# Index tiles for two halves by one transfer, and 25 rows of target scores in place of 22, in a graph attention kernel

## The reference, cut to what matters

```python
def gat_layer(feat, src, dst, W, a, gamma, beta):
    msg = feat @ W
    attn_src = msg @ a[:dh]
    attn_dst = msg @ a[dh:]
    scores = leaky_relu(attn_src[src] + attn_dst[dst], 0.2)
    e = exp(scores - scores.max())
    denom = segment_sum(e, dst, num_segments=n) + 1e-10
    out = segment_sum(msg[src] * (e / denom[dst])[:, None], dst, num_segments=n)
    ...
head_outs = [gat_layer(feat, src, dst, W_heads[h], ...) for h in range(8)]
x = gat_layer(concatenate(head_outs), src, dst, W_out, ...)
```

## Time and profile before

| | |
|---|---|
| median of 3 runs | 9308.34 us (9302.91 to 9314.57) |
| span of the profiled execution, first to last instruction | 7890.3 us |
| what the median has beyond this span | 1418.0 us |
| POOL busy, share of the span | 5124.5 us, 65% |
| DVE busy | 4825.2 us, 61% |
| PE busy | 5464.8 us, 69% |
| G0 (gathers start to next phase) | about 186 to 2296 us |
| G1 | about 2828 to 4990 us |

### The profile page before, as it was taken

One profiled execution on the slowest core, in us unless ns is written; L12 is line 12 of the kernel. 1 busy time (PEld: TensorE's weight loads), 2 busy tenths in 40 slices (PEclk: granted clock), 3 DMA queues, 4 the chain that ended last, 5 costly groups with the idle time before them and its releaser, 6 DMA issues.

```text
span 7890.3 us, 195306 instructions
## 1 busy us (share of the span) xinstructions
PE 5464.8 (69%) x50500; PEld 3952.8 (50%) x50501; DVE 4825.2 (61%) x14588; ACT 3085.2 (39%) x7615; POOL 5124.5 (65%) x4726
## 2 busy tenths in 40 slices
PE   3767677777773746777776777435878874888887
PEld 3655556565651336666666666323444442444444
DVE  7555555555556556666666666575666663555555
ACT  2111111111121135555555555413555552666665
POOL 1776767676740157777777777025887784777777
PEclk9977675656555855555555555567999996999999
DMA  3223232323233532222222222033555553544444
GB/s 122 57 56 77 56 77 56 77 56 77 56 76 125 148 47 52 52 51 51 51 51 51 51 51 51 12 91 95 124 124 125 124 125 92 120 116 118 118 118 107
DMA packets 600102, 647.29 MB, mean 82 GB/s; under 512 B 331121, under 2 KB 490355, under 8 KB 599665
## 3 DMA queue, kind: packets, MB, share of 16 engines
q0 software_dynamic: 190000, 384.58, 23.9%
q1 hardware_dynamic: 338379, 238.04, 10.4%
q10 hardware_dynamic: 71640, 23.81, 1.2%
HBM read 562.39 MB, written 83.23 MB: 82 GB/s over the span
## 4 chain that ended last, share of the span: by engine, by line
DVE 27%; issue 19%; POOL 15%; DMA 14%; PE 13%; DVEq 5%; ACT 3%; SPq 3%; ACTq 1%; POOLq 0%
POOL acc L659 8%; POOL rows L639 7%; DMA acc<-list_dst 7%; PE psa L1407 4%; PE psc L1366 3%; DMA rows<-t_gat,idx 2%; DVE acc L1729 2%; DVE acc L1781 1%; DMA acc<-in_x 1%; DVEq L619 1%; DMA acc<-y_d 1%; DVE acc L1728 1%; ACT ohb L1120 1%; PE psc L1498 1%; DVE s_m L1837 1%
## 5 line engine op out<-in xcount | busy, mean ns | idle before, releaser
L639 POOL DMA_INDIRECT rows<-t_gat,idx x3168 | 3142.8, 992 | 1189.8 <-issue 903.3
L659 POOL DMA_INDIRECT acc<-t_part,acc x1400 | 1826.6, 1305 | 546.6 <-issue 460.2
L1407 PE MATMUL psa<-rhs,rows 128*128 128x176 f32 (+1 forms) x6336 | 1713.1, 431 | 23.2 <-DVEq L1922 12.2
L1217 ACT ACTIVATE acc<-psa 128x384 bf16<-128x384 f32 x3200 | 1290.2, 506 | 884.7 <-PE psa L1481 765.8
L1407 PEld LDWEIGHTS psa<-rhs,rows 128*128 128x128 f32 x6336 | 1497.2, 311 | 132.0 <-DVEq L1922 83.2
L1481 PE MATMUL psa<-den,rhs 125*32 125x384 bf16 x12800 | 785.2, 343 | 191.4 <-ACT acc L1217 149.8
L1128 ACT ACTIVATE wgt<-s_d 128x64 f32<-128x64 f32 (+1 forms) x396 | 93.8, 237 | 1625.5 <-DVE s_d L1838 1610.8
L1122 ACT ACTIVATE oht<-psc 22x1024 bf16<-22x1024 bf16 x402 | 407.3, 1013 | 783.9 <-PE psc L1366 730.4
L1395 PE MATMUL psc<-oh,wgt 128*8 128x22 f32 (+1 forms) x6336 | 290.2, 205 | 552.1 <-ACT wgt L1128 543.8
L1071 ACT ACTIVATE acc<-stg,acc 128x128 bf16<-128x128 f32 x1818 | 552.9, 387 | 198.2 <-issue 116.0
L1481 PEld LDWEIGHTS psa<-den,rhs 125*32 125x32 bf16 x12800 | 285.6, 97 | 641.9 <-ACT acc L1217 412.7
(11 more groups left out here) (348 smaller groups left out, 7870.4 us busy)
## 6 DMA issues: line engine op xcount, KB each, us to landing
rows<-list_src SPq DMA_DIRECT2D x200, 500.0 KB
rows<-t_gat,idx POOLq DMA_INDIRECT x3168
acc<-y_d SPq DMA_DIRECT2D x50, 1000.0 KB, 5.0
y_d<-stg SPq DMA_DIRECT2D x100, 250.0 KB, 2.8
acc<-t_part,acc POOLq DMA_INDIRECT x1400
acc<-t_sage SPq DMA_DIRECT2D x300, 62.5 KB
adw<-win_d SPq DMA_DIRECT2D x820, 2.2 KB
adw<-win_d SPq DMA_DIRECT2D x788, 0.4 KB
```

The source lines that it names most:

```text
L639: eng.indirect_dma_start(rows[:, j, 0:spec["width"]], None, spec["table"], bass.IndirectOffsetOnAxis(ap=idx[:, j:j + 1], axis=0)).then_inc ...
L659: eng.indirect_dma_start(h_prow[u][:, t, :], None, t_parts[layer], bass.IndirectOffsetOnAxis(ap=h_idx[u][:, t:t + 1], axis=0)).then_inc(h_ ...
L1217: eng.activation(h_rows[:, g, :], psa[:, g % 4, 0:D3], ACT.Copy).then_inc(hyb["ev"], 1)
L1407: last = eng.matmul(sums(half, q, h), rows[:, slot * TH + j, 0:D], right, start=(j == 2 * q), stop=(j == 2 * q + 1))
```

## The change

One transfer now loads the indices of two slots (16 tiles, 64 bytes for each partition), issued in the odd slot after the rows of both have landed. Each semaphore `idx_in` stands for two slots, and POOL waits for it at the even slot only. The windows of `adw` are loaded with 25 rows (`WINL`); PE still uses the first 22. The tables in memory get three more rows at their end for it.

```diff
 WIN = 22
+WINL = 25
...
-        adw = sb("adw", [WIN, 2, PAIRS, 3 * K0], BF16)
+        adw = sb("adw", [WINL, 2, PAIRS, 3 * K0], BF16)
...
-                        eng.wait_ge(idx_in[slot], i * 16)
+                        if slot % 2 == 0:
+                            eng.wait_ge(idx_in[slot // 2], i * 16)
...
             def load_idx(slot, b):
-                eng.dma_start(idx[:, slot * TH:slot * TH + TH],
-                              src_t[:, ds(tile_at(spec, b, slot), TH)]).then_inc(idx_in[slot], 16)
+                eng.dma_start(idx[:, slot * TH:(slot + 2) * TH],
+                              src_t[:, ds(tile_at(spec, b, slot), 2 * TH)]).then_inc(idx_in[slot // 2], 16)
...
-                        eng.dma_start(adw[:, half, q, 0:3 * k], spec["window"][ds(at + s0, WIN), :]).then_inc(adw_in[half], 16)
+                        eng.dma_start(adw[:, half, q, 0:3 * k], spec["window"][ds(at + s0, WINL), :]).then_inc(adw_in[half], 16)
...
-                    eng.wait_ge(rows_in[spec["name"]][slot], value(eng, nb) * (16 * TH))
-                    load_idx(slot, eng.snap(nxt[1], min_val=0, max_val=(2 * SB - spec["slots"]) // spec["unit"]))
+                    if slot % 2:
+                        for read in (slot - 1, slot):
+                            eng.wait_ge(rows_in[spec["name"]][read], value(eng, nb) * (16 * TH))
+                        load_idx(slot - 1, eng.snap(nxt[1], min_val=0, max_val=(2 * SB - spec["slots"]) // spec["unit"]))
...
-            for slot in range(spec["slots"]):
+            for slot in range(0, spec["slots"], 2):
                 load_idx(slot, first)
...
-                        last = eng.matmul(p_adx[0:EP, j * k:(j + 1) * k], oht[:, j, :], adw[:, half, j // 2, r * k:(r + 1) * k],
+                        last = eng.matmul(p_adx[0:EP, j * k:(j + 1) * k], oht[:, j, :], adw[0:WIN, half, j // 2, r * k:(r + 1) * k],
```

More of the change, by code:

```diff
@@ L41 @@
 NW = N + WIN
+NWL = N + WINL
 HP = H // 2
@@ L190, in gnn_kernel @@
         list_idx = dram("list_idx", (NT, EP, TP), I32)
-        win0_d = dram("win0_d", (NW, 3 * K0), BF16)
-        win1_d = dram("win1_d", (NW, 3 * K1), BF16)
+        win0_d = dram("win0_d", (NWL, 3 * K0), BF16)
+        win1_d = dram("win1_d", (NWL, 3 * K1), BF16)
         bnd0_d = dram("bnd0_d", (NP_, NT * H))
@@ L434, in gnn_kernel @@
         bn_ready = sem("bn_ready")
-        idx_in = [sem(f"idx_in{i}") for i in range(RING)]
+        idx_in = [sem(f"idx_in{i}") for i in range(RING // 2)]
         rows_in = {p: [sem(f"rows_in_{p}{i}") for i in range(n)] for p, n in (("g0", RING), ("g1", RING), ("s0", 2), ("s1", 2))}
@@ L885, in sp_pass @@
                 list_load(c)
-            for slot in range(spec["slots"]):
-                eng.wait_ge(idx_in[slot], value(eng, ni) * 16)
+            for slot in range(0, spec["slots"], 2):
+                eng.wait_ge(idx_in[slot // 2], value(eng, ni) * 16)
             eng.sem_inc(alone, 1)
@@ L954, in store_windows @@
                 store(table[0:N, :].rearrange("(t p) c -> p t c", p=NP_), nw3[:, :, 0:3 * k])
-                store(table[N:NW, :], nw3[0:WIN, 0, 0:3 * k])
+                store(table[N:NWL, :], nw3[0:WINL, 0, 0:3 * k])
             load(pairs_i, dst.rearrange("(p n) -> p n", p=SB))
@@ L996, in _ @@
             eng.dma_start(bnd0_d, bnode).then_inc(win_out, 16)
-            eng.dma_start(win0_d[N:NW, :], nw3[0:WIN, 0, 0:3 * K0]).then_inc(win_out, 16)
+            eng.dma_start(win0_d[N:NWL, :], nw3[0:WINL, 0, 0:3 * K0]).then_inc(win_out, 16)
             eng.dma_start(win0_d[0:N, :].rearrange("(c p t) k -> p c (t k)", p=NP_, t=TC),
```

## The result

The changed kernel takes 9481.83 us (median of 5 runs, 9473.83 to 9502.58), the kernel before, run beside it, 9312.49 us (5 runs, 9302.91 to 9319.52). The ratio is 1.0186, with a 95% interval of 1.0174 to 1.0198: slower by 169 us. I had forecast 9310 us and no change.

The account below looks back on a forecast made before the run. POOL was taken to bound G0, and DVE's chain with the list building, narrowly, G1. Terms of -0.7 and +2.8 us gave +2.1 us on the 7890.3 us span; with 1418.0 us carried over, 9310 us, 8-in-10 range 9281 to 9338.

Parts of the forecast that it names:

- I carry the difference over unchanged: Whole kernel: the 1418.0 us by which the runs' median exceeds the profile's span stay the same after the change.
- G1, "worth 0": Pass G1, row buffers full: later index tiles of even slots cost 0 us.
- Its rows still land two halves before DVE wants them: G1: POOL's gathered rows stay early enough for DVE despite late indices, so 0 us.
- the moment of the index issue hangs on DVE: G1: through the list wait, the issue comes once for two halves at DVE's pace; part of the 0 us argument.
- Such a delay doesn't add up: G1: even if indices are 0.4 us late, POOL needs 21.2 us and is in time for the next; 0 us.
- the margin of 0.4 us: G1, even slot: indices issued at 4006.3 us land at 4008.1 us, 0.4 us before POOL wants them.
- Rival C: G1: late indices make POOL the limit, a further 0.5 us for two halves, 49 us slower, 9359 us; 5%.
- G0's restarts, +2.8 us: G0 after a flush: POOL gets slot 0's indices 0.7 us late, four times; +2.8 us (+1.2 to +5.2).
- 25 rows, -0.7 us: Window loads: each issue 0.03 us cheaper, 0.12 us for a front, counted at four restarts and two pass starts.
- A: G0: gathers move off VectorE's two-input instructions, 31 us faster, 9279 us; 10%.
- B: G0, similarly G1: gathers move onto another two-input VectorE instruction, +30 us over 200 halves of G0, 9340 us; 8%.
- D: Index loads: the removed transfers had been in the way, 428 us faster, 8880 us; 1%.

Follow-up runs that it names:

- e2: The changed kernel with windows back at 22 rows, leaving one index transfer for two slots; 9347.44 us, ratio 1.0191 to the kernel before.
- e1: The kernel before, unchanged, run and profiled again; 9168.02 us, ratio 1.0004.
- r2: The changed kernel as it is, run again on another chip; 7904.63 us, ratio 0.9996 to the kernel before.
- q1: The changed kernel with 22-row windows, plus a bare drain on POOL after every fourth gather of G1; 8897.89 us, ratio 1.1268 to the kernel before.
- t1: The changed kernel with 22-row windows, plus a 300-element memset after every fourth gather of G1; 8188.22 us, ratio 1.0378 to the kernel before.
- e3: The kernel before with windows of 25 rows, index transfers as before; 9167.56 us, ratio 0.9995.
- e4: The kernel before with windows of 32 rows, index transfers as before; 9172.82 us, ratio 1.0003.
- p3: The changed kernel with 22-row windows, its one index transfer moved ahead of the next front's windows; 9173.50 us, ratio 0.9999 to the kernel before.
- p4: The kernel before, still two index transfers and semaphores, both issued late in the odd slot where the change has its one; 9335.35 us, ratio 1.0181.
- p1: The changed kernel with 22-row windows, plus three drains and memsets after every fourth gather of G1; 9872.87 us, ratio 1.0765 to the kernel before.

## Why the prediction was wrong

**The reading of the profile.** The first failed step is "I carry the difference over unchanged". The 1418.0 us were not outside the instructions: they were G0, G1 and the SAGE stages themselves, in runs that take 1.16 to 1.18 times as long as those of kind B. All durations, gaps and slacks that the prediction used were those of kind B, and the time to be forecast was of kind A. The hint was in the table: 1418.0 us outside all instructions, which I put there without a reason. The profiled execution of the changed kernel has 1.6.

**G1, "worth 0".** This is the step that the result overturned; it measured +167 us on kind A, and nothing on kind B. Its argument had three parts. "Its rows still land two halves before DVE wants them" held: DVE waits for no row. That the moment of the index issue hangs on DVE and comes once for two halves at DVE's pace fits: in e2 it stands 23 to 26 us behind DVE's L1721 in every pair. "Such a delay doesn't add up" fell: in each pair of halves the late POOL has its gathers going on over PE's transposes for longer, ACT goes on 1.7 us later, and G1 is longer by as much: DVE, whose chain is the limit, waits behind ACT (L1733). The margin was off as well: I had the transfer land 1.8 us after its issue and 0.4 us ahead of its need; from issue to gather it takes 2.6 us in e2. On kind A the even slot's indices are issued some 23.5 us into a pair of halves (counted from DVE's L1721, L1716 before) where they stood at 17.5 us, and POOL stands for 4.3 us (median) where it stood for 2.1. On kind B, where I had reckoned it, the transfer takes as long, so the margin of 0.4 us was not there either, and yet G1 did not get longer. (By my own sum 2.6 us would have been 0.3 us late, not the 0.4 that I wrote.) The zero came out there by the other half of the argument, POOL's lead and DVE's pace, and in part by luck. Even with the profile of e1 the argument would have missed the cost, for it asked only whether rows come late, not what POOL's gathers hold up.

**Rival C** named the place (late indices in G1) and the sign, at 5% and +49 us. Its mechanism was another: POOL does not become the limit, for DVE waits for no rows in e2's G1.

**G0's restarts, +2.8 us.** On kind B the mechanism is as described. The timeline of r2:

```profile
1079.37 0.36 SPq L810 DMA_DIRECT2D idx<-in_src_t  x1
...
1082.01 0.94 POOL L642 DMA_INDIRECT rows<-t_gat,idx  x1 [20.84 <-DMA idx<-in_src_t]
```

From issue to gather it takes 2.64 us where I had put 2.0, 1.8 to land and 0.2 for POOL to react. The gap is 20.84 us against 19.15, and the four gaps together grow from 78.9 to 83.5 us, 4.6 in place of 2.8 and inside the bounds of 1.2 to 5.2. In q1 and t1, whose G0 is that of the index part too, the gaps come to 84.7 and 84.9 us, so nearer to 6 and a little beyond those bounds; their G0 takes 2116.4 and 2116.9 us where the old profile has 2110.0. That is under 0.1% of the time, and no ratio shows it. The term was sized too low by the landing, 1.8 us.

**25 rows, -0.7 us.** The issue of a 25-row window takes, in r2 (ns, min/median/max):

```profile
L853 SPq DMA_DIRECT2D adw<-win_d x1608: 262/269/349, 189.6 to 4975.5; - x179
```

0.026 us less than the 22-row issue, where I had 0.03, and worth nothing that shows (e3, 0.9995; e4, 1.0003). The later landing that I had left to the range doesn't show either.

**Rivals A, B and D.** G0's half did not move: in r2 it has 291 gathers in 370 us, as the earlier trace rows has 292. The busy time of a gather there is 0.967 us for 0.963, so few of them can have moved off or onto VectorE's instructions: A was to take 0.02 us off each, B to add as much. D's 206 spared transfers gave nothing back on either kind of chip (p3, 0.9999; r2, 0.9996). The advice of the Trainium skill (DMA: Bandwidth & Descriptors, Rules for kernel authors) to coalesce small transfers thus neither helps nor hurts for these index tiles; what hurts, on kind A, is the later issue that the merging brought with it, and p3 shows the merging without it.

**What stays open.** That late indices cost 167 us on kind A is shown by p3 and p4. That the cost stands between the end of PE's transposes and ACT's copy is shown by four traces, 166 of 167 us in e2 and 153 of 154 in p4. That PE's signal is held there by the run of gathers rests on the traces alone: ACT's copy follows the last gather of the run in 288 of 290 cases, but p1's wait may have vanished for another reason, the semaphore records of the first half of a run of eight go against the simple form of N, and the test with short pauses was not made on kind A. Why the two kinds differ, and whether the kind belongs to the chip, nothing here tells. No version beat both kernels.

## What to carry to other kernels

Compare the span of the profile with the time of the runs before anything else. In every profile here whose own execution was timed they differ by less than 2 us. If the difference is much larger, the profile may show another condition than the one that is timed, and each slack read from it may be gone; say so in the range, or forecast for both. When a transfer is merged, look where the merged one is issued, not how many are saved: keep it at the place of the earliest that it replaces. And an engine that is halves ahead can still cost time by when it works, not only by when it is done.

## What the hardware showed unexpectedly

- The same program takes 7889 to 7909 us on six chips, 9168 and 9174 us on two others and 9312 us in the runs of the result, with nearly the same busy times. Between the first and last gather, G1 is longer by 24% (2620.9 for 2115.3 us) and G0 by 26%, the stretch between them by 2%. The granted clock of G1 is 0.50 in both.
- On the slower kind, PE's transposes that end within a run of gathers are followed by ACT's copy only 1.9 to 2.9 us after the start of the run's last gather. Signals of PE within runs of four are late by 2.8 us in the median, and in e2 those in the second half of a run of eight by 2.7 to 6.1 us.
- On the other kind PE's signals are 0.01 us late in the median, in runs of over 300 gathers.
- With a drain on POOL behind a gather the next gather starts 2.6 us later at least and 3.0 us in the median (q1), where a plain gap is 0.30 us.
